# Preln transformer layer on one core: GpSimd scales the normalized rows of the projection, the weight work goes in single pieces, and the end of the attention stage is reordered

## The reference

```python
def _layernorm(x, axis=-1, eps=1e-05):
    m = jnp.mean(x, axis=axis, keepdims=True)
    v = jnp.var(x, axis=axis, keepdims=True)
    return (x - m) / jnp.sqrt(v + eps)

x = x + attn(_layernorm(x), Wq, Wk, Wv, Wo)     # x: 4 x 2048 x 256, float32
x = x + ffn(_layernorm(x), fast_b, w_fc, w_proj, u, v, gate)

# attn: q, k, v = x @ W.T, 16 heads of 16; a key is seen where |i - j| <= 128 or i == 0 or j == 0
logits = einsum('bhqd,bhkd->bhqk', q, k) / 4;  out = softmax(masked logits) @ v;  return out @ Wo.T
# ffn: bitlinear(x, w) = x @ (tern(w / scale) * scale).T, scale = mean |w| per row, tern = clip(round(.), -1, 1)
h = bitlinear(x, w_fc) + gate * (x @ v.T @ fast_b.T @ u.T)
r = maximum(h, 0);  return bitlinear(r * r, w_proj)
```

## Time and profile before

| | |
|---|---|
| median of 3 runs | 1242.32 us (1239.93 to 1242.99) |
| the profiled execution | 1241.55 us, of which its span is 1239.8 us |
| PE busy / DVE busy | 1161.0 us (94%) / 1027.8 us (83%) |
| ACT busy / POOL busy | 798.6 us (64%) / 695.4 us (56%) |
| projection: first turn to last turn on PE | 25.0 to 187.1 us from the span's start |
| tail of the projection | to about 228 us |
| attention stage | to about 871 us |
| feed stage | to the end |

### The profile page before, as it was taken

How to read it: one execution, slowest core, us unless ns; L and a number is a source line. 1 busy time by engine, 2 the same in 40 slices (tenths; PEclk the granted TensorE clock), 3 DMA queues, 4 the chain that set the end, 5 groups by cost and what they waited for, 6 DMA issues and landing times.

```text
span 1239.8 us, 26392 instructions
## 1 busy us (share of the span) xinstructions
PE 1161.0 (94%) x9051; PEld 765.2 (62%) x9051; DVE 1027.8 (83%) x3253; ACT 798.6 (64%) x1321; POOL 695.4 (56%) x928
## 2 busy tenths in 40 slices
PE   3998888589999999999999999997999999999997
PEld 3887776234444444444444444445888888889886
DVE  5899996588888888888888888885688888888885
ACT  2666555157777777778777877776565465465564
POOL 2544443437777776777777777676344244343343
PEclk7999998679999999999999999998999999999999
DMA  2789764474436644466436754314031131131200
GB/s 93 203 264 288 244 223 169 107 152 108 122 81 145 142 112 115 106 137 146 122 86 127 155 130 107 102 39 154 1 119 52 52 103 52 57 97 52 68 19 35
DMA packets 141254, 145.23 MB, mean 117 GB/s; under 512 B 23084, under 2 KB 134720, under 8 KB 141120
## 3 DMA queue, kind: packets, MB, share of 16 engines
q1 hardware_dynamic: 141120, 143.55, 43.5%
HBM read 91.74 MB, written 50.95 MB: 115 GB/s over the span
## 4 chain that ended last, share of the span: by engine, by line
PE 65%; DVE 6%; SPq 5%; issue 2%; POOL 1%; DMA 1%; ACT 1%; DVEq 0%; POOLq 0%
PE e_psum L1278 14%; PE e_psum L1320 14%; PE e_psum L1298 12%; PE e_psum L1587 5%; PE e_psum L1589 5%; SPq L1108 3%; PE e_psum L1568 3%; PE e_psum L1567 3%; PE e_psum L1016 2%; DVE n_stats L129 2%; DVE f_x L1686 2%; PE e_psum L1572 1%; PE e_psum L1536 1%; PE e_psum L202 1%; PE e_psum L203 1%
## 5 line engine op out<-in xcount | busy, mean ns | idle before, releaser
L1416 DVE CUSTOM_DVE_ANT_0 a_masked<-e_psum,a_band 128x387 f32<-128x387 f32 (+1 forms) x1024 | 502.7, 536 | 73.6 <-PE e_psum L1278 67.9
L1372 ACT ACTIVATE a_weights<-e_psum 128x1024 f32<-128x1024 f32 x384 | 385.5, 1022 | 111.4 <-PE e_psum L1298 111.2
L1278 PE MATMUL e_psum<-e_k,e_q 96*128 96x387 bf16 (+1 forms) x1024 | 328.1, 332 | 15.1 <-DMA e_q<-q_parts 11.2
L1177 POOL TENSOR_SCALAR_AFFINE_SELECT a_weights<-a_weights 128x1024 f32<-128x1024 f32 x256 | 275.6, 1089 | 52.3 <-ACT a_weights L1372 52.3
L1298 PE MATMUL e_psum<-e_q,e_k 128*128 128x384 bf16 (+2 forms) x1408 | 271.5, 278 | 6.8 <-DMA e_q<-a_shift 5.6
L1628 POOL TENSOR_TENSOR f_square<-f_relu 128x512 f32<-128x512 f32 x128 | 145.0, 1134 | 209.9 <-ACT f_relu L1617 198.3
L1278 PEld LDWEIGHTS e_psum<-e_k,e_q 96*128 96x128 bf16 x1024 | 93.7, 97 | 202.8 <-DVE a_max L1416 103.3
L1320 PE MATMUL e_psum<-a_weights,a_v 128*17 128x384 f32 (+2 forms) x2816 | 208.1, 393 | 0.3
L1298 PEld LDWEIGHTS e_psum<-e_q,e_k 128*128 128x128 bf16 x1408 | 136.6, 99 | 65.3 <-DMA e_q<-a_shift 7.0
L1587 PE MATMUL e_psum<-w_w_t,f_square_hi 128*128 128x256 f32 x512 | 128.9, 287 | 5.6 <-DVE f_square_lo L1674 5.6
L1589 PE MATMUL e_psum<-w_w_t,f_square_lo 128*128 128x256 f32 x512 | 125.9, 281 | 0.0
(11 more groups left out here) (205 smaller groups left out, 2025.0 us busy)
## 6 DMA issues: line engine op xcount, KB each, us to landing
k_parts<-p_k_parts SPq DMA_DIRECT2D x96, 129.0 KB, 2.8
e_k<-k_parts SPq DMA_DIRECT2D x64, 193.5 KB, 3.7
e_k<-k_parts SPq DMA_DIRECT2D x192, 64.5 KB, 3.4
q_parts<-p_q_parts SPq DMA_DIRECT2D x96, 128.0 KB, 3.7
e_q<-q_parts SPq DMA_DIRECT2D x64, 192.0 KB, 3.4
e_q<-q_parts SPq DMA_DIRECT2D x192, 64.0 KB, 3.2
v_ones<-p_va SPq DMA_DIRECT2D x16, 544.0 KB, 3.7
p_x<-in_x SPq DMA_DIRECT2D x16, 512.0 KB, 5.4
```

Of the source, the lines that this page charges most:

```text
L1177: pool.affine_select(out=blocks, in_=blocks, compare_op=ALU.is_ge, fill=0.0, base=0, pattern=[[0, NQ // 2 * HEAD_COLS // P // CUT_STEP], [ ...
L1278: pe.matmul(turn[TURN_OF_TILE[j] % TURN_BANKS][:, lo:hi], qw[ux.q][0:SLOT_ROWS, h, t * P:t * P + P], kt[ux.hq][0:SLOT_ROWS, h, start + lo: ...
L1372: act.activation(pe_w[:, us.upar, c * CHUNK:(c + 1) * CHUNK], score[c % 2][:], ACT.Exp).then_inc(s_exp, 1)
L1416: dve.tensor_tensor_reduce(out=masked[:, ux.upar, h, t:t + hi - lo], in0=bank[:, lo:hi], in1=band[:, lo:hi], scale=1.0, scalar=NEG, op0=AL ...
```

## The change

In the projection the scaling (`norm.scale`) goes from DVE, in the step of `LN`, to POOL, in the step of `LT`, as the first thing of POOL's step, ahead of the low parts. rstd is kept twice, by the parity of the group, and a semaphore of its own (`s_scaled`) tells PE and SP that the rows are scaled. DVE keeps the five instructions of rstd.

The weight work is spread anew: sums of w_fc in slots 2 to 5, scales in 6, u in 7 and 8, the eight ternary pieces of w_fc in the middle slots 10 to 24, sums of w_proj in 13 and 15, its scales in 17 and 19, its first three ternary pieces in the middle slots 26, 28 and 30, the other five after the sweep behind `dve_low`. No step has two ternary pieces. The loads are moved from groups 4, 6 and 8 to groups 2, 4 and 7. `pe_w2(n)` waits for 2(n+1) pieces, not for all eight.

At the end of the attention stage DVE does x1 and the statistics of group 0 at j == 4, ahead of the denominators of unit 61, and the low parts of group 1's turned output ahead of the scaling of group 0. POOL does the power ahead of the first cut of the last unit. PE does the turn of the scaled rows and the attention projection of group 1 at the end of its last step, behind the six `sum_block` calls.

```diff
@@ -118,10 +118,10 @@
         self.sd = sb("stddev", [P, 2, TB])
         self.r0 = sb("rstd_first", [P, TB])
         self.t0 = sb("newton", [P, TB])
-        self.rs = sb("rstd", [P, TB])
+        self.rs = sb("rstd", [P, 2, TB])
         self.exponent = sb("exponent", [P, TB])
-        self.s_step, self.s_sd, self.s_back, self.s_power = (
-            (outer or ctx).enter_context(nc.semaphore(f"{name}_{n}")) for n in ("step", "sd", "back", "power"))
+        self.s_step, self.s_sd, self.s_back, self.s_scaled, self.s_power = (
+            (outer or ctx).enter_context(nc.semaphore(f"{name}_{n}")) for n in ("step", "sd", "back", "scaled", "power"))
 
     def front(self, v, x, q):
         par, base = q.par, q.g * 3
@@ -139,13 +139,9 @@
         a.wait_ge(self.s_step, q.g * 3 + 3)
         a.activation(self.sd[:, q.par, :], self.ve[:, q.par, :], ACT.Sqrt).then_inc(self.s_sd, 1)
 
-    def back(self, v, x, xn, q):
-        self.rstd(v, q)
-        self.scale(v, x, xn, q, range(TB))
-
     def rstd(self, v, q):
 
-        par, base = q.par, q.g * 6
+        par, base = q.par, q.g * 5
         v.wait_ge(self.s_sd, q.g + 1 - self.powers)
         v.reciprocal(self.r0[:], self.sd[:, par, :]).then_inc(self.s_back, 1)
         v.wait_ge(self.s_back, base + 1)
@@ -155,7 +151,7 @@
         v.wait_ge(self.s_back, base + 3)
         v.tensor_scalar(self.t0[:], self.t0[:], -0.5, 1.5, ALU.mult, ALU.add).then_inc(self.s_back, 1)
         v.wait_ge(self.s_back, base + 4)
-        v.tensor_tensor(self.rs[:], self.t0[:], self.r0[:], ALU.mult).then_inc(self.s_back, 1)
+        v.tensor_tensor(self.rs[:, par], self.t0[:], self.r0[:], ALU.mult).then_inc(self.s_back, 1)
 
 
 
@@ -184,15 +180,12 @@
     def scale(self, v, x, xn, q, blocks):
 
         par = q.par
-        v.wait_ge(self.s_back, q.g * 6 + 5)
+        v.wait_ge(self.s_back, q.g * 5 + 5)
         for t in blocks:
-            ins = v.tensor_scalar(xn[:, t, :], x[:, t, :], self.mv[:, par, t, 0:1], self.rs[:, t:t + 1],
+            ins = v.tensor_scalar(xn[:, t, :], x[:, t, :], self.mv[:, par, t, 0:1], self.rs[:, par, t:t + 1],
                                   ALU.subtract, ALU.mult)
         if TB - 1 in blocks:
-            ins.then_inc(self.s_back, 1)
-
-    def done(self, q):
-        return q.g * 6 + 6
+            ins.then_inc(self.s_scaled, 1)
 
 
 def three_pass(pe, out, lhs_hi, lhs_lo, rhs_hi, rhs_lo):
@@ -313,7 +306,7 @@
 
             def body(at):
                 if q := at(0):
-                    wait(sp, norm.s_back, (q.g - 4) * 6 + 6)
+                    wait(sp, norm.s_scaled, q.g - 4 + 1)
                     sp.dma_start(xb[:, q.ring], x_v[bass.ds(q.g, 1)].rearrange("a p t d -> (a p) t d")
                                  ).then_inc(s_x[q.ring], DMA)
                     weights.load(sp, q.g)
@@ -362,6 +355,9 @@
                 pool.wait_ge(s_mask, count[1] + 2 + b)
 
             def body(at):
+                if q := at(LT):
+                    wait(pool, s_t, (q.g - 2) * KT + KT)
+                    norm.scale(pool, xb[:, q.ring], xn[:, q.par], q, range(TB))
                 if q := at(LP):
                     for u in range(2 * KT):
                         pool.wait_ge(s_mid, q.g * 4 + u + 1)
@@ -420,7 +416,7 @@
                 def turn():
 
                     if q := at(LT):
-                        pe.wait_ge(norm.s_back, norm.done(q))
+                        pe.wait_ge(norm.s_scaled, q.g + 1)
                         for k in range(KT):
                             wait(pe, s_lo, (q.g - 1) * KT + k + 1)
                             for t in range(TB):
@@ -625,8 +621,7 @@
                         dve.wait_ge(s_x[t.ring], (t.turn + 1) * DMA)
                         norm.front(dve, xb[:, t.ring], t)
                 if q := at(LN):
-                    wait(dve, s_t, (q.g - 2) * KT + KT)
-                    norm.back(dve, xb[:, q.ring], xn[:, q.par], q)
+                    norm.rstd(dve, q)
                 if q := at(LP):
                     weights.dve_part(dve, 2 * q.g + 1)
 
@@ -645,6 +640,8 @@
                                         over_bank[:, b * H:(b + 1) * H].unsqueeze(1).broadcast_to([P, NB, H]), ALU.add)
             ins.then_inc(s_rv, 1)
             weights.dve_low(dve)
+            for n in range((2 * G - weights.TERN2) // 2, 4 * KT):
+                weights.dve_ternary2(dve, n)
             dve.wait_ge(s_rpe, 3)
             dve.wait_ge(s_mask, MASKS)
             dve.reciprocal(rden[:], sum_bank[:, HD:VW]).then_inc(s_rv, 1)
@@ -766,16 +763,16 @@
 
     def load(self, sp, g):
         with self.nc.allow_non_contiguous_dma(reason="16 by 16, turned"):
+            if g == 2:
+                sp.dma_start(self.w1_in[:], self.w_fc.rearrange("(m p) k -> p m k", p=P)).then_inc(self.s_w1in, DMA)
             if g == 4:
-                sp.dma_start(self.w1_in[:], self.w_fc.rearrange("(m p) k -> p m k", p=P)).then_inc(self.s_w1in, DMA)
-            if g == 6:
                 sp.dma_start(self.u_in[:], self.u.rearrange("(m p) r -> p m r", p=P)).then_inc(self.s_in, DMA)
...
-            if g == 8:
+            if g == 7:
                 sp.dma_start(self.w2_in[:], self.w_proj.rearrange("(m p) k -> p m k", p=P)).then_inc(self.s_w2in, DMA)
 
     def pool_fill(self, pool):
@@ -783,7 +780,7 @@
 
 
 
-    SUMS1, SCALES1, U, TERN1, SUMS2, SCALES2, TERN2 = 4, 8, 9, 11, 19, 21, 23
+    SUMS1, SCALES1, U, TERN1, SUMS2, SCALES2, TERN2 = 2, 6, 7, 10, 13, 17, 26
 
     def dve_part(self, dve, i):
         if self.SUMS1 <= i < self.SUMS1 + 4:
@@ -805,22 +802,25 @@
                             self.u_hi[:].bitcast(F32).unsqueeze(2).broadcast_to([P, MH, 3, RANK]))
             dve.tensor_tensor(self.u_rows[:, :, 3, 0:RANK], self.u_div[:], self.u_hi[:].bitcast(F32), ALU.subtract
                               ).then_inc(self.s_u, 1)
-        elif self.TERN1 <= i < self.TERN1 + MH:
-            m = i - self.TERN1
-            self.dve_ternary(dve, self.w1_in[:, m, :], self.half1[:, m:m + 1], self.nhalf1[:, m:m + 1], self.s_tern1, m)
-        elif self.SUMS2 <= i < self.SUMS2 + KT:
-            self.dve_sums(dve, self.w2_in, self.s_w2in, self.mag2, i - self.SUMS2, 1)
+        elif i == self.SUMS2 or i == self.SUMS2 + 2:
+            self.dve_sums(dve, self.w2_in, self.s_w2in, self.mag2, (i - self.SUMS2) // 2, 1)
         elif i == self.SCALES2:
             self.dve_scales(dve, self.mag2, self.half2, self.nhalf2, HID, KT, self.DONE1)
-        elif i == self.SCALES2 + 1:
+        elif i == self.SCALES2 + 2:
             dve.wait_ge(self.s_dve, self.DONE2)
             for m in range(KT):
                 ins = dve.tensor_scalar(self.mag_diag[:, m, :], self.ident[:], self.mag2[:, m:m + 1], None, ALU.mult)
             ins.then_inc(self.s_mag, 1)
-        elif self.TERN2 <= i < self.TERN2 + 8:
-            m, c = divmod(i - self.TERN2, 4)
-            self.dve_ternary(dve, self.w2_in[:, m, c * D:(c + 1) * D], self.half2[:, m:m + 1], self.nhalf2[:, m:m + 1],
-                             self.s_tern2, MH + 4 * m + c)
+        elif self.TERN1 <= i < self.TERN1 + 2 * MH and i % 2 == 0:
+            m = (i - self.TERN1) // 2
+            self.dve_ternary(dve, self.w1_in[:, m, :], self.half1[:, m:m + 1], self.nhalf1[:, m:m + 1], self.s_tern1, m)
+        elif i >= self.TERN2 and i % 2 == 0:
+            self.dve_ternary2(dve, (i - self.TERN2) // 2)
+
+    def dve_ternary2(self, dve, n):
+        c, m = divmod(n, KT)
+        self.dve_ternary(dve, self.w2_in[:, m, c * D:(c + 1) * D], self.half2[:, m:m + 1], self.nhalf2[:, m:m + 1],
+                         self.s_tern2, MH + n)
 
     def dve_sums(self, dve, w, landed, mag, m, count):
         dve.wait_ge(landed, DMA)
@@ -908,7 +908,7 @@
         ins.then_inc(self.s_pt, 1)
 
     def pe_w2(self, pe, n):
-        pe.wait_ge(self.s_tern2, 8)
+        pe.wait_ge(self.s_tern2, KT * (n + 1))
         pe.wait_ge(self.s_pc, 4 + n)
         for i in range(2):
             for m in range(KT):
@@ -1212,6 +1212,8 @@
                     pool.tensor_tensor(num[:, uo.upar], turned[:, uo.upar, :, :, 0:HD], t0[:, uo.n % 3], ALU.add
                                        ).then_inc(s_num, 1)
                 if us:
+                    if us.n == UNITS - 1:
+                        feed.norm.power(pool, Group(0))
                     cut(us, 0, 0)
                 if uo:
                     pool.wait_ge(s_num, uo.n + 1)
@@ -1223,8 +1225,6 @@
                                        ALU.mult).then_inc(s_o, 1)
                 if us:
                     cut(us, 0, 1)
-                    if us.n == UNITS - 1:
-                        feed.norm.power(pool, Group(0))
                     cut(us, 1, 0)
                     cut(us, 1, 1)
 
@@ -1342,7 +1342,7 @@
                         feed.pe_attention(pe, Group(0))
                     if us and us.n == UNITS - 1 and j == TILES - 1:
                         feed.pe_turn_o(pe, Group(1))
-                    if up and up.n == UNITS - 1 and j == 4:
```

(10 more changed lines are left out.)

4 lines of the change are left out of this document (2 added, 2 removed).

## The result

The changed kernel took 1256.47 us (median of 4 runs, 1255.66 to 1258.44), the kernel before, on the same chip, 1241.59 (1239.93 to 1242.99). The ratio is 1.0123, with a 95% interval of 1.0104 to 1.0142: it is slower by 15 us where 15 us less were forecast.

What follows compares the result with a forecast made beforehand. DVE was taken to bound the projection's steps, after PE early on. Projection -9.9 and end of the attention stage -5.0 sum to -14.9 us, from 1242.32 to 1227 us; range 1221 to 1233.

Steps and rivals of the forecast that it cites:

- What bounds the kernel now: Projection: the bound passes from PE to DVE, with steps of 11.42 us where PE needs 9.73.
- POOL: four scalings of 128x256 ... I take 0.45: Projection: one scaling on POOL costs 0.45 us, between 0.27 and 0.632, so 1.8 us for four.
- The prediction's other estimate, 0.69: POOL's scaling priced at twice DVE's 0.35 us by the Trainium skill: 0.69 us each, total 1232 us.
- Does PE wait for them?: Projection: scaling ends 4.9 us behind the low parts, turn due 4.32 behind, so 0.6 late; fits in steps of 9.73.
- The slower rival: Projection: POOL's scaling is the bound, a step at least 6.7 + 4s; s = 1.25 gives 1251 us; chance 0.05.
- The first turn ... +0.4: Projection's start: the first turn waits for POOL's 1.8 us instead of DVE's 1.38, +0.4 us.
- The slots: Projection: sums in middle slots cost nothing, scales and u give two steps of 10.39, nine ternary steps take 10.2 us.
- 2.9 us off a chain that is 1.7 too long: Projection: DVE loses 2.08 us of scaling and a 0.85 piece per step; end slot and first `rest` stop counting.
- The rule on the shared port: Projection: two-input DVE and SBUF-reading POOL instructions block each other; L848 wins when first, steps 10.0, sum 1.8 us lower.
- Five pieces behind the sweep, hidden: Behind the projection sweep: five pieces, 4.5 us on DVE, covered by PE's sums of row 0 for over 10 us.
- Loads and queues at nothing: Projection: moved weight loads and SP's wait for x's buffer one step later cost nothing.
- End of the attention stage, -5.0: Reordered end: turn and projection of group 1 end at 866.2 against 871.2, -5.0 us, between -3 and -5.9.

Runs made afterwards that it cites:

- end_pieces: Changed kernel with all scaling on DVE, single ternary pieces in end slots, w_proj's sums and scales in middle slots: 1226.31 us, ratio 0.9872.
- no_key0: Changed kernel with key 0 copied on POOL for the first batch alone: 1248.49 us, ratio 1.0047.
- half_cols: Changed kernel with POOL's scaling in the projection on 128 of the 256 columns, both operations and scalars kept: 1235.95 us, ratio 0.9954.
- one_op: Changed kernel with POOL's scaling in the projection cut to one operation with one per-partition scalar: 1235.77 us, ratio 0.996.
- pool2_dve2: Changed kernel with the scaling shared, two of the four blocks on DVE and two on POOL: 1232.34 us, ratio 0.9925.
- pool0_dve4: Changed kernel with all four blocks scaled on DVE, single weight pieces and reordered end of the attention stage kept: 1234.81 us, ratio 0.995.
- drain_only: Kernel before with only the reordered end of the attention stage: 1234.77 us, ratio 0.9953.
- proj_only: Changed kernel with the end of the attention stage as before, so the projection half alone: 1261.01 us, ratio 1.0158.
- end_halves: All scaling on DVE, ternary pieces in end slots, and w_proj's load split in two, at groups 5 and 7: 1225.54 us, ratio 0.9879.

## Why the prediction was wrong

- **What bounds the kernel now** was read rightly. DVE held the steps at 11.4, and with DVE relieved in the right place (end_pieces) steps of 9.7 appear.
- **The step that failed: "POOL: four scalings of 128x256 ... I take 0.45", with 0.632 as the bound "from above".** It measured 1.225, and the bound failed with it. The rows that gave 0.27 and 0.632 are other kinds of instruction: L1177 handles 1024 columns in 1.089 us, 1.06 ns each, while this one takes 3.3 ns a column. Rows of the same engine bounded nothing here, because their operation was another. The Trainium skill (GPSIMD Engine Reference, Engine selection) calls one-input work on GpSimd roughly line rate against VectorE; no run here agrees, the same instruction being 0.345 us on DVE and 1.225 on POOL, with 0.924 for its simplest form. The prediction's other estimate, 0.69, is too low as well.
- **"Does PE wait for them?"** The path was right and its input wrong. The slower rival had the same terms: "a step is at least 6.7 + 4s from turn to turn", slower by 0.3% from s = 1.17. With 1.225 it gives 11.56, measured 11.4. It had a chance of 0.05 because 1.17 was "nearly twice the two-input row", which compared it with the wrong row; what it named for itself, two operations and per-partition scalars, are by the runs 0.22 and twice 0.08 us, and the rest is the price of the kind.
- **What the rival left out** is 8.6 us: 9.75 + 14 x 11.42 would be 169.6 from first to last turn, against 178.2. The copy of key 0 puts 0.5 us on four steps, and at those turns the clock fell in the changed kernel, 1.5 us more each. no_key0, without three of the copies and of the falls, is 6.3 shorter there, where 3 x 2.0 are expected (the rest of its 8.0 lies ahead of the first turn, 1.2, and behind the last). The rival's 1251 for s = 1.25 had 175.5 from first to last turn, where it was 178.2, and left the first turn as the forecast had it.
- **"The first turn ... +0.4"** was +4.3. Of this 3.45 is the same term (4.83 for 1.38), and 0.7 lies ahead of it: the statistics of the first group begin at 20.86 instead of 20.20.
- **The slots.** "Uncontended the step would be PE's 9.73, fully contended 10.39", with 10.2 taken for the nine steps with a ternary piece, was too low as well, a second term that failed. The changed kernel didn't test it: POOL holds its steps, and in six of the eight middle slots between 60 and 187 us the piece ran uncontended, as at 124.85 us in the rows below this list. Without any scaling on DVE, half_cols (s = 0.80) took 10.9 us on average for the nine steps that were put at 10.2, and one_op (s = 0.92) 10.9; pool2_dve2 took 10.7. What they would be at s = 0.45 no run shows. By the prediction's own terms a dear piece and the scaling add up: the low parts end 6.07 us behind the turn (79.99 - 73.92) and the scaling 4.9 behind them, which is 11.0 and not 10.39. The long step of half_cols is this sum, 6.3 + 5.9 = 12.2.
- **"2.9 us off a chain that is 1.7 too long"** counted the 0.85 of the cheap piece as gone. In pool0_dve4, where the scaling stays on DVE, the pieces took 1.12 + 1.23 and their steps 10.8 to 12.0, because 10 of the 11 pieces left in the sweep are dear, where 8 of 16 were before. Its one step of 10.42 is, like the 10.39, the step with the scales, the first in which DVE falls behind: from 72.77 to 83.96 (rows below) DVE's row took 11.2 us, while the turn came only 10.39 later, out of DVE's lead.
- **The rule on the shared port** (the Trainium skill, SBUF — State Buffer, Who interferes with whom) agrees in these kernels: the same two instructions take 0.41 + 0.48 where they run first or alone, and 1.1 + 1.2, at most 1.41 each, beside POOL. The forecast used it to say that L848 would more often run ahead; in half_cols it did in every second step.
- **Five pieces behind the sweep, hidden:** right. They ran from 230.50 to 235.6 and DVE then waited 7.2 us for other things.
- **Loads and queues at nothing:** no wait for x or for a store shows in the changed kernel, whose steps are long. In the faster kernels the load of w_proj does cost, 2.2 us of waiting and a long step, because SP's issues fill a step of 9.7. The price of a load thus depends on the length of the steps around it.
- **End of the attention stage, -5.0:** right in size and by its steps, from the last exponentials. With the delay of 20.2 taken off, the last cut ends at 858.7 (858.8 forecast), the scaling at 862.35 (862.3), `pe_low_rank` begins at 866.2 (866.2). The newton steps did stand beside the cuts, six of eight at 0.56 to 1.05 us. drain_only gives -5 by itself.

The ternary piece in the changed kernel's middle slot, on DVE, and then, of the kernel before, the first `rest` behind the step of rows 3:

```profile
124.85 0.41 DVE L848 TENSOR_TENSOR z_below<-z_w_in,z_nhalf 128x256 f32<-128x256 f32 x1
125.29 0.48 DVE L850 SCALAR_TENSOR_TENSOR z_w_in<-z_w_in,z_half,z_below 128x256 f32<-128x256 f32 x1
```

```profile
83.96 1.28 DVE L611 SCALAR_TENSOR_TENSOR p_rest<-p_bank,p_q_parts 128x512 f32<-128x512 f32 x2
```

The change by its parts, from the medians: POOL's scaling costs 21.7 us (1256.5 - 1234.8, the changed kernel against pool0_dve4), the single pieces bring nothing (pool0_dve4 against drain_only, 1234.8 both), and the drain brings 5 to 6.

## What to carry to other kernels

Before work moves to an engine that has never run that instruction in this kernel, price it as unknown: the nearest row of another operation is no upper bound, and a threshold such as "slower from 1.17 us" deserves a chance of its own until one run has shown the duration. Work is cheap or dear by its slot; of two equal pieces take away the one that runs beside the other engine on the path, not the one that is easier to move. And price a load by its issue too, where the queue's issues already fill the step: cutting it in two doubled that price.

## What the runs showed that was not expected

- POOL's `tensor_scalar` on 128x256 float32 takes 0.92 us (one operation, one scalar), 1.07 (two operations, constants) or 1.225 (two of each), and 0.80 on 128x128 with two of each.
- Two copies of 0.20 us on POOL cost 2 us of a step where POOL was the bound and PE's wait grew from 1.5 to 2.0 us: 0.5 by themselves, and 1.5 because the granted clock was 0.50 for some of the next microseconds. The same wait left the clock alone in proj_only at 98.00 and in one_op at 176.90.
- Instructions of 2 to 8 columns on DVE are held for a whole instruction of POOL: 1.05 for 0.16 us in the newton steps, 0.86 and 1.08 for the scales of w_proj.
- SP's queue took 1.14 us to issue a load of 1 MB and 1.13 to issue one of 512 KB (end_pieces, end_halves).
